# Sparse attention block: 76 instead of 64 of the 128 query blocks gather their selected rows from memory

## The chip, the cores and the metric

One NeuronCore of a Trainium2 chip. The metric is the device time of one execution of the whole kernel in microseconds (us), as the median of several runs. One execution was also recorded by the hardware profiler; every row below is from it.

## The reference, cut to what matters

The model is x = x + 0.5 FFN(LN(x)); x = x + Attention(LN(x)); x = x + 0.5 FFN(LN(x)) on x of shape (2, 1024, 128). Only the attention is touched by the change. Its heart:

```python
I = einsum('bts,h->bts', relu(einsum('bthd,bsd->bths', q_i, k_i)), idx_w)
I = where(local, inf, I); I = where(causal, -inf, I)     # local: last 64 positions
_, idx = top_k(I, 96)                                    # 64 local ones and 32 chosen ones
key_c = (c_kv @ W_uk)[bi, idx]; value = (c_kv @ W_uv)[bi, idx]
kr_sel = (x @ W_kr)[bi, idx]; key_r = pope(kr_sel, angles_k)
scores = (q_c . key_c + q_r . key_r) * scale
out = softmax(scores) @ value
```

Each query attends to its 64 last positions and to 32 earlier ones that are picked by an index score (positions below 96 are taken in a fixed order where fewer exist).

## The kernel before, in words

**Stages.** The span of 1686.8 us holds an FFN stage, the attention, and the FFN stage again. The attention has a start of its own up to about 687 us (projections, selection for the first tiles), and then a loop over 128 blocks of 16 queries up to about 1139 us. The change lies in the loop and, with one list, in that start.

**Blocks, tiles, phases.** A tile is 128 queries, 8 blocks k = 0 to 7. A batch has 8 tiles: the near ones are its tiles 0 to 3, the far ones 4 to 7. The loop has 8 phases q = 0 to 7 (q = 0 to 3 for batch 0) of 16 blocks. A phase takes one far tile and one near tile (`far_tile`, `near_tile`: near tiles 3, 2, 1, 0 in turn), in pairs of blocks: two far, two near, two far, and so on (`place`). So r, the place in the phase, is 2, 3, 6, 7, 10, 11, 14, 15 for the near blocks, and 14 and 15 are their k = 6 and 7.

**The 32 chosen rows of a block** reach the transposed keys (`pe_keys`) in one of two ways. Far blocks: GpSimd issues 4 indirect DMAs (L750) that fetch rows of `kv_rows` from memory into one of GR = 6 buffers `G`, and TensorE transposes the four (L1136). Near blocks: VectorE makes one-hot matrices (`dve_onehot`, L1886), one for each 128 candidate positions (`chunks`: 1 to 4), and TensorE multiplies a three-part bf16 table of all keys with them (L1142, three matmuls for each one-hot); for the value product the fetched rows are then turned back by four transposes (L1173 in `pe_turned`), which gathered blocks don't need.

**The loop** is software pipelined. In its iteration i, TensorE does in this order: `pe_turned`(i) (L1170), `pe_keys`(i+3), `pe_scored`(i+2) (L1155, L1158, L1161), the index units that are due, `pe_mixed`(i) (L1186, L1189). VectorE: `dve_inverse`(i+1) (L1908), `dve_keys`(i+3) (L1894), `dve_least`(i+2) (L1903), `dve_onehot`(i+5), every fourth time `dve_attended` (L1918), and the selection steps due. ScalarE: `act_turned`(i) (L1422), `act_queries` (L1412), `act_scaled`(i+1) (L1435), `act_weights`(i+2) (L1429), the index units due (`act_index`). Each engine takes them strictly in this order; I count iterations by TensorE's L1170. The key work of near blocks at r = 14 and 15 is therefore in the iterations at r = 11 and 12.

**Selection** for a tile list s = 2q (far) or 2q + 1 (near) is spread over the phase before its own. `INDEX` lists TensorE's units with their iteration: index scores (L1123, four heads for each half of 512 positions) and, for far lists, a transpose of the finished list (half None, L1117), whose result ScalarE copies with four instructions to `IDX` (L1393), from which GpSimd's gathers read. All units share two PSUM banks: `pe_index` lets unit v wait until ScalarE has handled unit v-2.

```python
v = IX_AT[s, half, h]
if v >= 2:
    pe.wait_ge(ix_out, v - 1)
o = bank[v % 2]
```

With B = 16(q-1) - 4, far list 2q has its units at B-5 to B-2 and its transpose at B+7; near list 2q+1 has its scores at B+4 and B+5. `STEPS` lists VectorE's: "add0" and "add1" sum the heads (L1840), eleven steps find the 32 largest (L1871, L1873, L1875), "out" writes the list. So at r = 9 VectorE has the "out" of a near list and then "add0" of the next far list, and at r = 10 TensorE has two index units, of heads 2 and 3 of the second half. The near list goes through memory to all partitions (`sp_near`), for the one-hots. GpSimd's gather of far block d waits for the last use of its buffer (`ob_done` of the far block six earlier).

Of the kernel before, what the change touches and what calls it, by code (L numbers as in the profile page):

```python
# [16 lines left out]
P = 128  # L17
# [56 lines left out]
    return q, far, (far_tile if far else near_tile)(q), 2 * (r // 4) + r % 2  # L74


def position(d):

    q, k = divmod(d, 8)
    return q * PER + 4 * (k // 2) + k % 2  # L80


def chunks(tile, k):
# [4 lines left out]
def onehots():  # L88

    units = []  # L90
    for i in range(NB):
        q, far, tile, k = place(i)
        if not far:
            units += [(i, c) for c in range(chunks(tile, k))]
    return units

# [9 lines left out]
def index_units():  # L106

    units = []
    for q in range(PHASES):
        base = PER * (q - 1) - SHIFT  # L110
        for half in range(2):
            units += [(base - 5 + 2 * half + h // 2, 2 * q, half, h) for h in range(NIH)]
        units += [(base + 4 + h // 2, 2 * q + 1, 0, h) for h in range(NIH)]
        units += [(base + 7, 2 * q, None, None)]
    return sorted(units, key=lambda u: u[0])


# [9 lines left out]
    return sorted(steps, key=lambda u: u[0])  # L127


ONEHOTS = onehots()  # L130
OH_AT = {i: [n for n, u in enumerate(ONEHOTS) if u[0] == i] for i in range(NB)}
INDEX = index_units()
# [102 lines left out]
def build(nc, ins, const_ap, rot_ap, mask_ap, out):  # L235
# [10 lines left out]
    with ExitStack() as ctx:  # L246
# [55 lines left out]
        inverse = sb("inverse", [P, 3])  # L302
        best = sb("best", [P, NSEL])
        bidx = sb("bidx", [P, NSEL], U32)
        bidf = sb("bidf", [P, 2, NSEL])
        bidh = sb("bidh", [P, 2, NSEL], F16)
        near0 = sb("near0", [P, NSEL])
        IDX = sb("IDX", [P, PHASES, P // 4], U32)

        arena_at = -(-nc.sbuf_base // 32) * 32  # L310
# [134 lines left out]
        mus_done, qr_ready = sem("mus_done"), sem("qr_ready")  # L445
        q_placed = [sem(f"q_placed{i}") for i in range(2)]

        ix_done, ix_out, sc_used, far_ready, near_ready, idx_ready = (sem(n) for n in ("ix_done", "ix_out", "sc_used", "far_ready", "near_ready", "idx_ready"))
        idx_stored, oh_ready = sem("idx_stored"), sem("oh_ready")
        idxb_loaded = [sem(f"idxb_loaded{half}") for half in range(2)]  # L450
        gathered = [sem(f"gathered{i}") for i in range(GR)]
# [271 lines left out]
        def pool_sel(pool):  # L723
            pool_rstd(pool, 3)
            pool.wait_ge(x_ready, 1)
            pool.wait_ge(xn_ready, NG * 2)
            pool.memset(KVS[:, :, ROWKV:], 1.0)
            pool.drain()
            pool.memset(KL[0:P // 2, :, :], 0.0)
            pool.memset(KL[P // 2:, :, 0:LW], 0.0)  # L730
            pool.drain()
            pool.memset(RT[P // 2:, :], 1.0)
            pool.wait_ge(mask_loaded, 16)
            pool.drain()
            pool.tensor_copy(maskb[:, :, :].rearrange("p v n -> p (v n)"), MASKF)
            pool.drain()
            pool.memset(spare[:, 10:11], 0.0).then_inc(padded, 1)
            pool.wait_ge(kv_stored, 16 * B)
            for q in range(PHASES):
                for k in range(8):  # L740
                    d = 8 * q + k
                    if d == 4:
                        pool.wait_ge(qr_ready, 2 * 2 * B)
                    if d >= GR:
                        pool.wait_ge(ob_done, position(d - GR) + 1)
                    if k == 0:
                        pool.wait_ge(idx_ready, 3 * (q + 1))
                        pool.wait_ge(ix_out, IX_AT[2 * q, None, None] + 1)
                    for g in range(GB):
                        pool.indirect_dma_start(G[d % GR][:, g, :], None, kv_rows,  # L750
                                                bass.IndirectOffsetOnAxis(ap=IDX[:, q, k * GB + g:k * GB + g + 1], axis=0))\
                            .then_inc(gathered[d % GR], 16)

        def pe_turn(pe, tile, n, ready, base):

# [227 lines left out]
        def pe_sel(pe):  # L983
# [63 lines left out]
            pe_raw_queries(pe, 3)  # L1047
            pe_swap(pe, 2)
            pe_swap(pe, 3)
            for u in INDEX:  # L1050
                if u[0] < 0 and u[1] == 2:
                    pe_index(pe, u)
# [55 lines left out]
        def pe_index(pe, unit):  # L1108

            _, s, half, h = unit  # L1110
            v = IX_AT[s, half, h]
            if v >= 2:
                pe.wait_ge(ix_out, v - 1)
            o = bank[v % 2]
            if half is None:
                pe.wait_ge(far_ready, s // 2 + 1)
                pe.transpose(o[0:NSEL, 0:P], bidf[:, s // 2 % 2, :], ident).then_inc(ix_done, 1)  # L1117
                return
            tile = tile_of(s)
            b = tile // TB  # L1120
            r = slice((h % 2) * DH, (h % 2 + 1) * DH)
            lo, hi = half * BANK, min(scores_of(s), (half + 1) * BANK)
            pe.matmul(o[:, 0:hi - lo], QI[r, h // 2, tile * P:(tile + 1) * P], KI[r, b * L + lo:b * L + hi],  # L1123
                      start=True, stop=True).then_inc(ix_done, 1)

        def pe_keys(pe, x):

            q, far, tile, k = place(x)
            if x >= 2:
                pe.wait_ge(gts_ready, x - 1)  # L1130
            o = bank[4 + x % 2]
            if far:
                d = 8 * q + k
                pe.wait_ge(gathered[d % GR], 16 * GB * (d // GR + 1))
                for g in range(GB):
                    m = pe.transpose(o[:, g * P:(g + 1) * P], G[d % GR][:, g, :], ident)  # L1136
            else:
                b, n = tile // TB, chunks(tile, k)
                for c in range(n):
                    pe.wait_ge(oh_ready, OH_AT[x][c] + 1)  # L1140
                    for part in range(OHPARTS):
                        m = pe.matmul(o[:, :], TAB[part][:, 4 * b + c, :], OH[OH_AT[x][c] % OHR][:, :],  # L1142
                                      start=(c == 0 and part == 0), stop=(c == n - 1 and part == OHPARTS - 1))
            m.then_inc(gt_done, 1)
# [18 lines left out]
        def pe_turned(pe, x):  # L1163
# [4 lines left out]
                pe.wait_ge(pts_ready, x)  # L1168
            for part in range(2):
                m = pe.transpose(bank[6][:, part * P:(part + 1) * P], PB[x % 3][:, part * P:(part + 1) * P], ident)  # L1170
            if not far:
                for g in range(GB):
                    m = pe.transpose(bank[6][:, 2 * P + g * DC:2 * P + (g + 1) * DC],  # L1173
                                     GTS[x % 3][2 * DR:ROWKV, g * P:(g + 1) * P], ident[2 * DR:ROWKV, 2 * DR:ROWKV])
            m.then_inc(tp_done, 1)

        def pe_mixed(pe, x):
# [7 lines left out]
            pts = PTS[x % 2]  # L1185
            pe.matmul(o, KVS[:, tile, 2 * DR:ROWKV] if k >= 4 else KV64[:, tile, :], pts[:, 0:P], start=True, stop=True)  # L1186
            for g in range(GB):
                rows = G[(8 * q + k) % GR][:, g, 2 * DR:ROWKV] if far else pts[:, 2 * P + g * DC:2 * P + (g + 1) * DC]
                m = pe.matmul(o[:, g * STRIP:(g + 1) * STRIP], rows, pts[:, P + g * STRIP:P + (g + 1) * STRIP],  # L1189
                              start=False, stop=True, skip_group_check=True)  # L1190
            m.then_inc(ob_done, 1)
# [103 lines left out]
        def act_sel(act):  # L1295
# [49 lines left out]
            for n in range(B, 2 * B):  # L1345
                act_round(act, n)
                act_log(act, (MU[n % 2],)).then_inc(mu_log, 1)
            for u in INDEX:
                if u[0] < 0 and u[1] == 2:
                    act_index(act, u)  # L1350
# [32 lines left out]
        def act_index(act, unit):  # L1383
# [3 lines left out]
            act.wait_ge(ix_done, v + 1)  # L1387
            o = bank[v % 2]
            if half is None:
                q = s // 2  # L1390
                src = o[0:NSEL, 0:P].rearrange("p (g t) -> p t g", t=4)
                for t in range(4):
                    m = act.activation(IDX[t * NSEL:(t + 1) * NSEL, q, :], src[:, t, :], ACT.Copy)  # L1393
                    m.then_inc(ix_out if t == 3 else idx_ready, 1)
                return
            n = min(scores_of(s), (half + 1) * BANK) - half * BANK
# [17 lines left out]

        def act_turned(act, x):

            far = place(x)[1]
            act.wait_ge(tp_done, x + 1)
            if x >= 2:
                act.wait_ge(ob_done, x - 1)  # L1420
            n = 2 * P if far else 3 * P
            act.activation(PTS[x % 2][:, 0:n], bank[6][:, 0:n], ACT.Copy).then_inc(pts_ready, 1)  # L1422

        def act_weights(act, x):
# [401 lines left out]
        def dve_select(dve, unit):  # L1826
# [15 lines left out]
                                             ALU.mult, ALU.add).then_inc(sc_used, 2 if h == 1 else 1)  # L1842
                return
            if step == "out":
                f = bidf[:, q % 2, :]
                if s % 2 == 0:
                    if q >= 2:
                        dve.wait_ge(ix_done, IX_AT[s - 4, None, None] + 1)
                    dve.tensor_copy(f, bidx[:, :])
                    dve.drain()  # L1850
                    dve.tensor_scalar(f, f, float(tile // TB * L), None, ALU.add).then_inc(far_ready, 1)
# [4 lines left out]
                if tile % TB == 0:  # L1856
                    dve.tensor_copy(near0[:, :], bidx[:, :])
                    dve.drain()
                    dve.tensor_tensor(near0[:, :], near0[:, :], cst("keep"), ALU.mult)
                    dve.drain()  # L1860
                    dve.tensor_tensor(fh, near0[:, :], cst("fill"), ALU.add).then_inc(near_ready, 1)
                else:
                    dve.tensor_copy(fh, bidx[:, :]).then_inc(near_ready, 1)
                return
            r = slice(step // 3 * 8, step // 3 * 8 + 8)
            if step == 0:
# [10 lines left out]
        def dve_onehot(dve, x):  # L1877

            q, far, tile, k = place(x)
            if far:  # L1880
# [132 lines left out]
```

## Time and profile before

| | |
|---|---|
| median of 3 runs | 1689.7 us (1689.04 to 1690.89) |
| the profiled execution | 1688.96 us, its span 1686.8 us |
| PE (TensorE matmul) busy | 1401.3 us, 83% of the span |
| DVE (VectorE) | 1243.8 us, 74% |
| ACT (ScalarE) | 976.6 us, 58% |
| POOL (GpSimd) | 447.8 us, 27% |
| the 128-block loop | about 687 to 1139 us |

Busy time counts the latency of single instructions, and matmuls overlap: a row of nine matmuls of 395 ns each does not last nine times as long. Spacing, the distance from one step's start to the next's, is what counts on TensorE. "PEclk" is the clock granted to TensorE as a share of full speed. "Idle before" names what ended an engine's wait.

### The profile page before, as it was taken

The numbers are of one execution on the slowest core, as the hardware profiler recorded it, in microseconds if no ns is written. First come the engines' busy times: TensorE is split into PE (matmuls) and PEld (weight loads), VectorE is DVE, ScalarE is ACT, GpSimd is POOL, SyncE is SP. The second block draws the span as 40 slices with busy tenths as digits, with TensorE's granted clock in tenths as the row PEclk, the third lists the DMA queues.
The fourth block names the chain that finished last, engine by engine and source line by source line (L and its number), as shares of the span: only waits on it lengthen the run. The fifth ranks groups of instructions, "written<-read, shape, count | busy, mean of one in ns | idle before, by whom it ended". The sixth has DMA issues, their size and how long they took to land.

```text
span 1686.8 us, 31737 instructions
## 1 busy us (share of the span) xinstructions
PE 1401.3 (83%) x10664; PEld 915.3 (54%) x10664; DVE 1243.8 (74%) x2568; ACT 976.6 (58%) x1788; POOL 447.8 (27%) x751
## 2 busy tenths in 40 slices
PE   3599999799994754789999989996399999799994
PEld 2355554577773311456656655675255555577773
DVE  4578886698778577677878887754478887488787
ACT  2166666478883672346455555552166666488883
POOL 4122222100002023245455445622222233100000
PEclk9599999799997965899899999997599999799998
DMA  5211110022202244122122122212311110022200
GB/s 143 95 48 45 43 47 11 1 102 76 75 26 78 47 121 112 30 61 61 36 80 73 38 61 63 74 36 81 110 33 47 46 47 18 2 102 75 75 25 25
DMA packets 65020, 99.72 MB, mean 59 GB/s; under 512 B 21109, under 2 KB 44853, under 8 KB 62840
## 3 DMA queue, kind: packets, MB, share of 16 engines
q1 hardware_dynamic: 55254, 80.43, 15.5%
q0 software_dynamic: 8192, 16.79, 3.9%
q8 instruction: 75, 1.23, 0.3%
q10 hardware_dynamic: 1440, 0.80, 0.2%
q14 instruction: 59, 0.47, 0.1%
HBM read 73.39 MB, written 10.69 MB: 50 GB/s over the span
## 4 chain that ended last, share of the span: by engine, by line
PE 55%; DVE 13%; ACT 10%; DMA 6%; issue 6%; SPq 5%; DVEq 4%; ACTq 1%; POOL 0%; POOLq 0%
PE twin L973 8%; PE twin L963 5%; PE twin L827 5%; PE twin L1142 5%; PE twin L805 5%; DMA ffn<-arena 4%; PE twin L772 4%; ACT arena L1209 4%; DVEq L1830 2%; ACT experts L1279 2%; PE twin L1170 2%; PE twin L1158 2%; PE twin L1123 2%; PE twin L1186 2%; ACT arena L1277 2%
## 5 line engine op out<-in xcount | busy, mean ns | idle before, releaser
L1209 ACT ACTIVATE arena<-twin 128x1024 f32<-128x1024 f32 x288 | 293.8, 1024 | 172.7 <-PE twin L805 170.8
L750 POOL DMA_INDIRECT arena<-kv_rows,IDX x256 | 251.6, 983 | 309.9 <-PE twin L1189 151.0
L1478 DVE TENSOR_REDUCE arena<-twin 128x8 f32<-128x1024 f32 (+1 forms) x160 | 195.3, 1225 | 77.2 <-PE twin L772 42.9
L1277 ACT ACTIVATE arena<-twin,bias 128x512 f32<-128x512 f32 x256 | 184.9, 722 | 60.6 <-PE twin L963 60.6
L1527 DVE TENSOR_TENSOR experts<-arena,experts 128x512 fp32r<-128x512 f32 x256 | 170.1, 689 | 61.8 <-ACT experts L1279 60.5
L963 PE MATMUL twin<-experts,experts 128*128 128x512 f32 x768 | 197.0, 403 | 6.1 <-ACT experts L1279 6.1
L772 PE MATMUL twin<-ffn,ffn 64*128 64x128 f32 (+3 forms) x1152 | 154.8, 351 | 50.5 <-DMA arena<-arena 27.7
L1468 DVE TENSOR_REDUCE arena<-twin 128x2 f32<-128x1024 f32 x128 | 152.9, 1222 | 51.8 <-PE twin L772 48.4
L1279 ACT ACTIVATE experts<-twin,bias 128x512 fp32r<-128x512 f32 x256 | 186.2, 727 | 0.0
L973 PE MATMUL twin<-experts,experts 128*128 128x512 f32 x768 | 183.3, 390 | 1.0 <-DVE experts L1527 1.0
L711 POOL TENSOR_SCALAR_AFFINE_SELECT arena<-arena 128x256 f32<-128x256 f32 x256 | 99.6, 407 | 307.6 <-ACT arena L1209 307.6
L805 PE MATMUL twin<-ffn,ffn 64*128 64x128 f32 (+3 forms) x960 | 148.4, 373 | 27.7 <-DMA ffn<-arena 22.7
L963 PEld LDWEIGHTS twin<-experts,experts 128*128 128x128 f32 x768 | 143.2, 192 | 51.1 <-ACT experts L1279 23.7
L973 PEld LDWEIGHTS twin<-experts,experts 128*128 128x128 f32 x768 | 143.9, 188 | 32.9 <-issue 2.6
L827 PE MATMUL twin<-arena 128*32 128x128 f32 (+3 forms) x1920 | 159.2, 432 | 2.6 <-POOL arena L711 1.6
L645 POOL TENSOR_TENSOR rstd<-vareps,neghalf 128x8 f32<-128x8 f32 x14 | 23.4, 1674 | 511.7 <-DVE vareps L1457 511.7
L772 PEld LDWEIGHTS twin<-ffn,ffn 64*128 64x128 f32 x1152 | 96.7, 201 | 83.9 <-ACT arena L1209 36.1
L805 PEld LDWEIGHTS twin<-ffn,ffn 64*128 64x128 f32 x960 | 79.2, 188 | 109.0 <-issue 62.4
L1894 DVE TENSOR_TENSOR HN<-twin,RT 96x512 f32<-96x512 f32 x128 | 86.9, 680 | 59.1 <-PE twin L1142 51.4
L1429 ACT ACTIVATE ATT<-twin,col 128x256 f32<-128x256 f32 x128 | 60.6, 473 | 104.9 <-DVE col L1903 104.0
L1435 ACT ACTIVATE ATT<-ATT,inverse 128x256 f32<-128x256 f32 x128 | 64.6, 505 | 81.3 <-DVE inverse L1908 80.8
L1142 PE MATMUL twin<-XN,arena 128*128 128x512 bf16 x408 | 104.2, 395 | 0.2 <-DVE HN L1894 0.2
(258 smaller groups left out, 2186.6 us busy)
## 6 DMA issues: line engine op xcount, KB each, us to landing
arena<-wt_rows SPq DMA_DIRECT2D x16, 1024.0 KB, 4.8
arena<-in_L_ffn_w SPq DMA_DIRECT2D x32, 256.0 KB, 5.2
ffn<-q_rows SPq DMA_DIRECT2D x64, 128.0 KB
ffn<-k_rows SPq DMA_DIRECT2D x64, 128.0 KB
XT<-idx_rows SPq DMA_DIRECT2D x16, 512.0 KB, 4.1
q_rows<-ffn SPq DMA_DIRECT2D x8, 512.0 KB, 4.9
k_rows<-ffn SPq DMA_DIRECT2D x4, 1024.0 KB, 9.2
arena<-HN SPq DMA_DIRECT2D x32, 128.0 KB, 2.4
```

The source lines that it names most:

```text
L750: pool.indirect_dma_start(G[d % GR][:, g, :], None, kv_rows, bass.IndirectOffsetOnAxis(ap=IDX[:, q, k * GB + g:k * GB + g + 1], axis=0))\
L772: m = pe.matmul(bank[2 * slot + s][:, at * P:(at + blocks) * P], QB[buf][r, q * P:(q + 1) * P], KB[buf][r, k0 * P:(k0 + blocks) * P], star ...
L805: x = pe.matmul(bank[2 * slot + s][:, at * P:(at + 4 - p) * P], KB[buf][r, kc * P:(kc + 1) * P], QB[buf][r, (4 * g + p) * P:(4 * g + 4) * ...
L827: m = pe.matmul(bank[6][r:r + STRIP, p * P:], VS[buf][:, v:v + STRIP], PT[(UNITS * buf + u) % PT_RING][:, s, at * P:(at + 4 - p) * P], sta ...
L963: m = pe.matmul(bank[f][:, :], W1R[buf][w][:, f * P:(f + 1) * P], XR[x][:, tb * BANK:(tb + 1) * BANK], start=((w, x) == pairs[0]), stop=(( ...
L973: m = pe.matmul(bank[4 + k][:, :], W2R[buf][w][:, f, :], H1R[k][x][:, f, :], start=(f == 0 and (w, x) == pairs[0]), stop=(f == FC - 1 and ...
L1142: m = pe.matmul(o[:, :], TAB[part][:, 4 * b + c, :], OH[OH_AT[x][c] % OHR][:, :], start=(c == 0 and part == 0), stop=(c == n - 1 and part ...
L1209: act.activation(PT[(UNITS * buf + u) % PT_RING].rearrange("p s n -> p (s n)"), twin[2 * u % S_RING][:, :], ACT.Exp, scale=float(HD) ** -0 ...
L1277: act.activation(H1[tb % 2][:, f, :], bank[f][:, :], ACT.Gelu_apprx_tanh, bias=bias1[buf][:, f:f + 1])
L1279: act.activation(H1R[tb % 2][0][:, f, :], bank[f][:, :], ACT.Gelu_apprx_tanh, bias=bias1[buf][:, f:f + 1]).then_inc(gelu_done, 1)
L1478: dve.tensor_reduce(to, scores.rearrange("p (s t k) -> p s t k", s=2, t=to.shape[2]), AX_X, ALU.max).then_inc(max_done, 1)
L1527: dve.tensor_tensor(H1R[tb % 2][1][:, f, :], H1[tb % 2][:, f, :], H1R[tb % 2][0][:, f, :].bitcast(F32), ALU.subtract)\
```

## The change

Near blocks k = 6 and 7 of every near tile with at least two chunks there, that is near tiles 3, 2 and 1 of both batches (phases 0, 1, 2, 4, 5, 6), are gathered from memory as far ones are: 12 blocks more, 76 of 128. Their one-hots, table matmuls and the four transposes in `pe_turned` go. For this the near lists too are turned into row numbers: "out" of a near list makes them in `bidf` (with the batch's offset added), and each near list gets a transposing unit in `INDEX` and its four copies to `IDX`. The gathers run through one list `GATHERED`; their buffers are handed on from one gathered block to the one six places later in that list.

```diff
+def gathered_rows(i):
+    q, far, tile, k = place(i)
+    return far or (k >= 6 and chunks(tile, k) >= 2)
...
-        units += [(base + 7, 2 * q, None, None)]
+        units += [(base + 7, 2 * q, None, None), (base + (14 if q else 7), 2 * q + 1, None, None)]
...
+GATHERED = [i for i in range(NB) if gathered_rows(i)]
+G_AT = {i: d for d, i in enumerate(GATHERED)}
...
+            lists = set()
+            for d, i in enumerate(GATHERED):
+                q, far, tile, k = place(i)
+                s = 2 * q + (0 if far else 1)
...
+                if d >= GR:
+                    pool.wait_ge(ob_done, GATHERED[d - GR] + 1)
+                if s not in lists:
+                    lists.add(s)
+                    pool.wait_ge(idx_ready, 3 * (s + 1))
+                    pool.wait_ge(ix_out, IX_AT[s, None, None] + 1)
...
             pe_swap(pe, 3)
+            pe_index(pe, INDEX[IX_AT[1, None, None]])
...
-            if far:
-                d = 8 * q + k
+            if gathered_rows(x):
+                d = G_AT[x]
...
                 act_log(act, (MU[n % 2],)).then_inc(mu_log, 1)
+            act_index(act, INDEX[IX_AT[1, None, None]])
...
+                f = bidf[:, s % 4, :]
+                if q >= 2:
+                    dve.wait_ge(ix_done, IX_AT[s - 4, None, None] + 1)
+                dve.tensor_copy(f, bidx[:, :])
+                dve.drain()
+                if tile % TB == 0:
...
+                dve.tensor_copy(fh, f).then_inc(near_ready, 1)
+                dve.drain()
+                dve.tensor_scalar(f, f, float(tile // TB * L), None, ALU.add).then_inc(list_ready, 1)
                 return
```

In the `INDEX` that results, the transpose of near list 2q+1 (q from 1) falls into iteration 16q - 6, the place r = 10, and stands there ahead of the two index units of far list 2q+2.

## Rows read from the trace of the kernel before

**Rows 1.** The page's chain that ended last, by engine.
```profile
PE 55%; DVE 13%; ACT 10%; DMA 6%; issue 6%; SPq 5%; DVEq 4%; ACTq 1%; POOL 0%; POOLq 0%
```
**Rows 2.** Windows of iterations 113 to 116: us, then PE PEld DVE ACT POOL busy, PEclk.
```profile
1101.26:1103.44 2.18, 2.18 (x30) 1.70 (x27) 1.98 (x6) 1.37 (x5) 1.53 (x2) 1.00 0.32 79
1103.44:1106.14 2.70, 2.70 (x34) 2.01 (x32) 1.54 (x5) 1.76 (x6) 2.09 (x3) 1.00 0.29 76
1106.14:1109.00 2.86, 2.86 (x34) 1.91 (x31) 1.53 (x4) 1.45 (x5) 2.02 (x3) 1.00 0.32 76
1109.00:1111.39 2.39, 2.39 (x29) 1.64 (x26) 1.32 (x4) 1.57 (x6) 1.89 (x2) 1.00 0.33 78
```
**Rows 3.** Windows of iterations 75 to 77 of phase 4, same columns.
```profile
971.14:975.94 4.80, 4.80 (x42) 2.79 (x39) 2.63 (x8) 2.75 (x8) 2.93 (x4) 1.00 0.82 252
975.94:980.28 4.34, 4.34 (x38) 2.53 (x36) 2.87 (x7) 1.69 (x6) 0.00 (x0) 1.00 0.08 27
980.28:984.33 4.05, 2.26 (x31) 1.71 (x28) 3.78 (x8) 1.37 (x4) 2.84 (x3) 1.00 0.14 36
```
**Rows 4.** Timeline of iteration 74 (r = 10): start, us, engine, line; ScalarE's index unit last.
```profile
966.41 1.13 DVE L1886 TENSOR_SCALAR XN<-XT,const 128x512 bf16<-128x512 f16 x4
967.63 0.18 DVE L1863 CAST bidh<-bidx 128x32 f16<-128x32 uint32 x1
969.41 1.21 PE L1123 MATMUL twin<-arena 64*128 64x320 f32 x4
971.90 0.94 ACT L1400 ACTIVATE arena<-twin,aw 128x320 f32<-128x320 f32 x2
```
**Rows 5.** Timeline around iteration 67: a far list's transpose and its four copies.
```profile
942.84 0.27 PE L1117 MATMUL twin<-const,bidf 128*32 128x128 f32 x1
944.15 0.80 ACT L1393 ACTIVATE IDX<-twin 32x32 uint32<-32x32 f32 x4
```
**Rows 6.** DVE timeline of phase 4: its waits for near keys in iterations 75 and 76.
```profile
974.67 0.69 DVE L1894 TENSOR_TENSOR HN<-twin,RT 96x512 f32<-96x512 f32 x1 [2.01 <-PE twin L1142]
979.01 0.69 DVE L1894 TENSOR_TENSOR HN<-twin,RT 96x512 f32<-96x512 f32 x1 [0.69 <-PE twin L1142]
```
**Rows 7.** The same of phase 1 (iteration 27).
```profile
800.36 0.69 DVE L1894 TENSOR_TENSOR HN<-twin,RT 96x512 f32<-96x512 f32 x1 [2.18 <-PE twin L1142]
```
**Rows 8.** Timeline of phase 3, iterations 58 and 59.
```profile
908.54 0.59 PE L1123 MATMUL twin<-arena 64*128 64x192 f32 x4
909.65 0.44 PE L1170 MATMUL twin<-const,ATT 128*128 128x128 f32 x2
910.45 0.72 ACT L1400 ACTIVATE arena<-twin,aw 128x192 f32<-128x192 f32 x2
911.24 0.69 DVE L1894 TENSOR_TENSOR HN<-twin,RT 96x512 f32<-96x512 f32 x1 [0.50 <-PE twin L1142]
```
**Rows 9.** Chain of waits from 590 to 700 us: the near list's cast stands on it.
```profile
625.37 0.28 DVE bidh L1863
```
**Rows 10.** Timeline at the end of the attention's start: DVE's wait there.
```profile
678.95 1.57 DVE L1719 MEMSET HN<- 32x512 f32 x3 [2.83 <-DMA arena<-XN]
```
**Rows 11.** POOL timeline: first and last gather of the third-last pair of blocks (8 instructions).
```profile
1091.46 0.94 POOL L750 DMA_INDIRECT arena<-kv_rows,IDX  x1 [1.42 <-PE twin L1189]
1100.19 0.94 POOL L750 DMA_INDIRECT arena<-kv_rows,IDX  x1 [0.30 <-issue]
```
**Rows 12.** Windows of iterations 18 (phase 1) and 82 (phase 5), the same work.
```profile
764.81:768.88 4.07, 4.07 (x32) 2.90 (x32) 3.60 (x11) 3.15 (x10) 2.85 (x5) 0.60 0.21 50
999.77:1003.10 3.33, 2.84 (x31) 2.01 (x31) 3.24 (x11) 2.77 (x9) 2.42 (x4) 1.00 0.20 48
```
**Rows 13.** All gather instructions of L750 by source: duration min/median/max in ns.
```profile
L750 POOL DMA_INDIRECT arena<-kv_rows,IDX x256: 938/944/1897, 619.4 to 1110.3; - x128
```
**Rows 14.** The page's DMA issues: KB each, and us from issue to landing.
```profile
XT<-idx_rows SPq DMA_DIRECT2D x16, 512.0 KB, 4.1
arena<-HN SPq DMA_DIRECT2D x32, 128.0 KB, 2.4
```

More of the change, by code:

```diff
@@ L74, in place @@
     return q, far, (far_tile if far else near_tile)(q), 2 * (r // 4) + r % 2
-def position(d):
-    q, k = divmod(d, 8)
-    return q * PER + 4 * (k // 2) + k % 2
+def gathered_rows(i):
+    q, far, tile, k = place(i)
+    return far or (k >= 6 and chunks(tile, k) >= 2)
 def chunks(tile, k):
@@ L92, in onehots @@
         q, far, tile, k = place(i)
-        if not far:
+        if not gathered_rows(i):
             units += [(i, c) for c in range(chunks(tile, k))]
@@ L304, in build @@
         bidx = sb("bidx", [P, NSEL], U32)
-        bidf = sb("bidf", [P, 2, NSEL])
+        bidf = sb("bidf", [P, 4, NSEL])
         bidh = sb("bidh", [P, 2, NSEL], F16)
-        near0 = sb("near0", [P, NSEL])
         IDX = sb("IDX", [P, PHASES, P // 4], U32)
@@ L446, in build @@
         q_placed = [sem(f"q_placed{i}") for i in range(2)]
-        ix_done, ix_out, sc_used, far_ready, near_ready, idx_ready = (sem(n) for n in ("ix_done", "ix_out", "sc_used", "far_ready", "near_ready", "idx_ready"))
+        ix_done, ix_out, sc_used, list_ready, near_ready, idx_ready = (sem(n) for n in ("ix_done", "ix_out", "sc_used", "list_ready", "near_ready", "idx_ready"))
         idx_stored, oh_ready = sem("idx_stored"), sem("oh_ready")
@@ L738, in pool_sel @@
             pool.wait_ge(kv_stored, 16 * B)
-            for q in range(PHASES):
-                for k in range(8):
-                    d = 8 * q + k
[L742 to L752, printed above, removed]
+            lists = set()
+            for d, i in enumerate(GATHERED):
+                q, far, tile, k = place(i)
+                s = 2 * q + (0 if far else 1)
+                if d == 4:
+                    pool.wait_ge(qr_ready, 2 * 2 * B)
+                if d >= GR:
[4 more added lines that the diff above has]
+                    pool.wait_ge(ix_out, IX_AT[s, None, None] + 1)
+                for g in range(GB):
+                    pool.indirect_dma_start(G[d % GR][:, g, :], None, kv_rows,
+                                            bass.IndirectOffsetOnAxis(ap=IDX[:, s % PHASES, k * GB + g:k * GB + g + 1], axis=0))\
+                        .then_inc(gathered[d % GR], 16)
         def pe_turn(pe, tile, n, ready, base):
@@ L1115, in pe_index @@
             if half is None:
-                pe.wait_ge(far_ready, s // 2 + 1)
-                pe.transpose(o[0:NSEL, 0:P], bidf[:, s // 2 % 2, :], ident).then_inc(ix_done, 1)
+                pe.wait_ge(list_ready, s + 1)
+                pe.transpose(o[0:NSEL, 0:P], bidf[:, s % 4, :], ident).then_inc(ix_done, 1)
                 return
@@ L1131, in pe_keys @@
             o = bank[4 + x % 2]
-            if far:
-                d = 8 * q + k
+            if gathered_rows(x):
+                d = G_AT[x]
                 pe.wait_ge(gathered[d % GR], 16 * GB * (d // GR + 1))
@@ L1170, in pe_turned @@
                 m = pe.transpose(bank[6][:, part * P:(part + 1) * P], PB[x % 3][:, part * P:(part + 1) * P], ident)
-            if not far:
+            if not gathered_rows(x):
                 for g in range(GB):
@@ L1187, in pe_mixed @@
             for g in range(GB):
-                rows = G[(8 * q + k) % GR][:, g, 2 * DR:ROWKV] if far else pts[:, 2 * P + g * DC:2 * P + (g + 1) * DC]
+                rows = G[G_AT[x] % GR][:, g, 2 * DR:ROWKV] if gathered_rows(x) else pts[:, 2 * P + g * DC:2 * P + (g + 1) * DC]
                 m = pe.matmul(o[:, g * STRIP:(g + 1) * STRIP], rows, pts[:, P + g * STRIP:P + (g + 1) * STRIP],
@@ L1389, in act_index @@
             if half is None:
-                q = s // 2
                 src = o[0:NSEL, 0:P].rearrange("p (g t) -> p t g", t=4)
                 for t in range(4):
-                    m = act.activation(IDX[t * NSEL:(t + 1) * NSEL, q, :], src[:, t, :], ACT.Copy)
+                    m = act.activation(IDX[t * NSEL:(t + 1) * NSEL, s % PHASES, :], src[:, t, :], ACT.Copy)
                     m.then_inc(ix_out if t == 3 else idx_ready, 1)
@@ L1415, in act_turned @@
         def act_turned(act, x):
-            far = place(x)[1]
             act.wait_ge(tp_done, x + 1)
@@ L1420, in act_turned @@
                 act.wait_ge(ob_done, x - 1)
-            n = 2 * P if far else 3 * P
+            n = 2 * P if gathered_rows(x) else 3 * P
             act.activation(PTS[x % 2][:, 0:n], bank[6][:, 0:n], ACT.Copy).then_inc(pts_ready, 1)
@@ L1844, in dve_select @@
             if step == "out":
-                f = bidf[:, q % 2, :]
-                if s % 2 == 0:
[L1847 to L1851, printed above, removed]
+                f = bidf[:, s % 4, :]
[4 more added lines that the diff above has]
+                if tile % TB == 0:
+                    dve.tensor_tensor(f, f, cst("keep"), ALU.mult)
+                    dve.drain()
+                    dve.tensor_tensor(f, f, cst("fill"), ALU.add)
+                    dve.drain()
+                if s % 2 == 0:
+                    dve.tensor_scalar(f, f, float(tile // TB * L), None, ALU.add).then_inc(list_ready, 1)
                     return
@@ L1855, in dve_select @@
                     dve.wait_ge(idx_stored, 16 * (q - 1))
[L1856 to L1863, printed above, removed]
+                dve.tensor_copy(fh, f).then_inc(near_ready, 1)
+                dve.drain()
+                dve.tensor_scalar(f, f, float(tile // TB * L), None, ALU.add).then_inc(list_ready, 1)
                 return
@@ L1879, in dve_onehot @@
             q, far, tile, k = place(x)
-            if far:
+            if gathered_rows(x):
                 return
```

## The prediction

> **What bounds the kernel now.** I read the page first. The chain that ended last lies on TensorE for 55% and on VectorE for 13%, on GpSimd not at all [rows 1]. So the question is what the 128-block loop makes of less TensorE work, and I read it iteration by iteration in windows that run from one first instruction of `pe_turned` to the next. Late in the loop, when selection is over, TensorE fills each window: 2.18 or 2.70 us for an iteration that transposes gathered rows, 2.86 or 2.39 us for one that builds near keys from one chunk [rows 2]. The two of each kind differ by 0.5 us: that is the value transposes L1173, which only a near block has. In phase 4 the iterations at r = 11 and 12, which build the keys of near blocks k = 6 and 7 from four chunks, last 4.80 and 4.34 us with TensorE full, and VectorE is busy for 2.63 and 2.87 us of them; the next one has TensorE busy for 2.26 of 4.05 us and VectorE for 3.78 [rows 3]. So TensorE bounds r = 11 and 12, VectorE bounds what follows, and both take work in strict order, so a delay at r = 10 or 11 is handed on to both. That is where I look closest, because the change also adds a unit at r = 10.
>
> **What is removed.** Three chunks more cost 4.80 - 2.86 = 1.94 us, so a chunk costs 0.65 us. With gathered rows, r = 11 and 12 take 2.70 + 2.18 = 4.88 us [rows 2]. Against 9.14 us for four chunks [rows 3] TensorE can give back 4.26 us in phases 0 and 4, 4.26 - 1.30 = 2.96 us in phases 1 and 5 (three chunks), 1.67 us in phases 2 and 6 (two): 17.8 us in all. The L1173 transposes at r = 14 and 15 give 0.5 us each, but only where TensorE bounds: in phase 6, 1.0 us. VectorE loses 36 one-hots; four took 1.13 us [rows 4], so 4, 3 or 2 of them stand at r = 9 and as many at r = 10. In r = 11 VectorE waited 2.01 us for the near keys in phase 4 and 0.69 us more in r = 12 [rows 6], and 2.18 us in phase 1 [rows 7]; what TensorE gives back is worth these waits and little more.
>
> **What is added at r = 10.** The near list's transpose is put ahead of the two index units there. Before, unit v waited for ScalarE to have done unit v-2, and with two units in an iteration those were units of the iteration before. With three, the last one waits for the list's unit of the same iteration. ScalarE comes to its index units only at the end of its own iteration, after `act_weights`: in iteration 74 TensorE issued the two units from 969.41 us on, the second at about 969.8, and ScalarE began them at 971.90 [rows 4]. It will now first make the four copies of the list, 0.80 us [rows 5]. Behind the waiting unit stand `pe_mixed` and the whole next iteration, and VectorE then waits for the next keys.
> - Phases 0 and 4: four one-hots go ahead of ScalarE's start (-1.13 us) and two small operations come in "out" (one takes 0.18 us and with its drain 0.26, so +0.52), so it starts at 971.3. 971.3 + 0.80 + 0.05 = 972.15, minus 969.8: TensorE stands 2.35 us. In r = 11 gathered keys reach VectorE 1.27 us into the iteration instead of 974.67 - 971.14 = 3.53 [rows 3, 6], 2.26 us saved, so VectorE is 0.1 us late there; the wait of 0.69 us in r = 12 goes. Net -0.6 us each, -1.2.
> - Phases 1 and 5: a stall of 2.3 us, a saving of 2.26 - 0.65 = 1.61 us, no second wait to save: +0.7, and 0.15 for the later scores. +0.85 us each, +1.7.
> - Phase 2: a stall of about 2.9 us (two one-hots fewer, but two operations more), a saving of 0.97 us and perhaps a second wait of the size of the 0.69: between +0.5 and +1.9. I take +1.0.
> - Phase 3 gathers nothing more, but has the added unit too. The two units start at 908.54 and about 908.7, ScalarE at 910.45 and then 0.5 later: 910.45 + 0.52 + 0.85 - 908.7 = 3.1 us. VectorE's only wait there was 0.50 us and was for the keys themselves [rows 8], so nothing absorbs it: +3.1 us.
> - Phase 6 has the list alone at r = 10, no stall: -1.67 - 1.0 + 0.2 for the transpose = -2.5 us.
>
> **GpSimd's supply.** Eight gathers took from 1091.46 to 1100.19 + 0.94 us, 1.25 us a step, so 10.0 us for a pair of blocks; four iterations take 10.1 us [rows 2, 11]. Before, a buffer came free 12 iterations ahead of its next block; after six gathered blocks in a row it is 8. The tightest place is r = 5 of phase 7: from the first release of the pair to the use of its second block are five iterations of 2.18, 2.18, 2.39, 2.39 and 2.18 us and 0.7 more, 12.0 us; the eighth gather starts 0.6 + 8.75 = 9.35 us after it. The trace has no row for a gather's landing. With 2.4 us it is in time, with 4.1 us [rows 14] it is 1.45 us late. I take the middle, +0.7 us. In the other phases iterations are 3.5 us and more, and the slack is above 4 us.
> Most gather instructions take 944 ns, the longest 1897 [rows 13]. The Trainium skill ("SBUF — State Buffer", section "SBUF: two separate sides") says that VectorE operations of certain modes lock GpSimd out of a shared port while it writes descriptors, which speaks against putting more gathers beside a full VectorE. By it the supply would cost nearer 1.45 than 0.7 us; by the rows few instructions are stretched, and they are in phases with slack.
>
> **The attention's start.** "out" of near list 0 stands on the chain as one cast of 0.28 us [rows 9] and becomes three operations: +0.5 us. The added transpose and copies (about 1 us) delay the selection for list 2, which ends in a wait of VectorE of 2.83 us for a DMA [rows 10]: hidden. If that cover were gone they would cost 1 us.
>
> **TensorE's clock.** Iteration 18 had a granted clock of 0.60, that is partly 1.2 GHz, and took 4.07 us; iteration 82, the same work at 1.00 (2.4 GHz), took 3.33 [rows 12]. Such falls come after iterations like 77, where TensorE is half idle. Work is removed and stalls are added ahead of just these, so I add two such falls, +1.5 us; the ends are 0 and 3.
>
> **Sum.** 0.5 - 1.2 + 1.7 + 1.0 + 3.1 - 2.5 + 0.7 + 1.5 = +4.8 us on the profiled execution of 1688.96 us (its span of 1686.8 and 2.2 around it), 1693.8 us. The median of the runs shown lies 0.7 us above that execution: 1694.5 us. With the ends of the terms (phases 0 and 4 -1.4 to +0.4 each, 1 and 5 +0.4 to +1.5, phase 2 +0.5 to +1.9, phase 3 +2.3 to +3.6, phase 6 and supply -2.5 to -1.0, start 0.3 to 0.8, clock 0 to 3), not all at one side, the forecast's own range is 1691 to 1699 us.
>
> **The rivals.**
> *Faster: the added unit doesn't hold TensorE.* If ScalarE reaches the list early, because VectorE, freed of the one-hots, lets it run ahead, the savings come through: 3.6 us in phases 0 and 4 (between the waits of 2.7 us of rows 6 and TensorE's 4.26), 2.5 in 1 and 5, 1.7 in 2, +0.2 in 3, and -1.8 and +0.5 as above: -15 us, 1674.7 us. For it: TensorE bounds and loses 17.8 us of work. Against: ScalarE was 2.1 us behind TensorE's second unit [rows 4], and the one-hots are worth only 0.6 us of that. It decides where that lag falls under about 0.5 us. Half of it would be 1684.
> *Slower still: the clock.* If each of the six stalls brings two iterations at the low clock, 6 x 2 x 0.74 = 8.9 us stand in place of 1.5: 1701.9 us. For it: TensorE's share of the time falls just ahead of its idle iterations. Against: phase 4 went through the same iterations at 1.00 throughout [rows 3]. The Trainium skill ("TensorE: Matmul & The Clock Gate", section "HAM oscillation — how this bites in real kernels") says that gaps between bursts of matmuls take the clock back again and again; by it this rival is the likelier one, by the rows 0.74 us a time is all it costs.
> *Slower: gathers late.* If every pair of phase 7 lands late by 1.45 us, 4.4 us stand in place of 0.7: 1698.2 us. It decides from a landing of 2.65 us on.
>
> **How the numbers follow.** Forecast 0.60, faster rival 0.17, clock 0.13, late gathers 0.06, 0.04 for a small gain or loss. No change is within 0.2%, 3.4 us, about what a measurement of this kernel can tell. The forecast's 4.8 us lie just above: 0.42 slower and 0.18 the same. The faster rival is 0.15 faster and 0.02 the same, both others slower, the rest the same: 0.15, 0.24, 0.61. The range goes from 1684, half of the faster rival, to 1701, most of the clock's.
>
> **What would show it.** In the new trace L1123 at r = 10 should have a wait on ScalarE's copies (L1393's line), 2.3 to 3 us, in phases 0 to 5 and not in 6; the windows r = 11 and 12 should be 2.7 and 2.2 to 2.5 us; L1886 should have 100 instructions and the gathers 304; phase 3 should be longer by 3 us, phase 6 shorter by 2. The prediction is wrong if phase 3 is not longer, or if GpSimd's gathers are waited for before phase 6.

## The result and the profile after

The changed kernel takes 1704.6 us in the median (1702.6 to 1708.2), the kernel before on the same chip 1690.1 us (1689.0 to 1690.9). The ratio is 1.0089, with an interval of 1.0069 to 1.0109: 14.6 us slower, where I had forecast 4.8 slower and a range up to 1701. The profiled execution took 1702.62 us with a span of 1700.9, the longer by 14.1 us. The first `pe_turned` is 1.04 us later than before, the loop is 11.5 us longer (441.4 to 452.9), and the rest 1.5 us.

The chain of the page, in the place of [rows 1], still lies on TensorE first:

```profile
PE 51%; DVE 16%; ACT 10%; DMA 7%; issue 7%; DVEq 4%; SPq 3%; POOL 1%; ACTq 0%; POOLq 0%
```

TensorE's waits in the loop: engine, line, releaser, us in total, times, the longest.

```profile
PE twin L1174 <- ACT ATT L1438: 31.0, 27, 2.4
PE twin L1127 <- ACT IDX L1397: 12.8, 6, 2.9
PE twin L1140 <- DMA arena<-kv_rows,IDX: 1.0, 1, 1.0
```

The second row is the predicted wait, which I call the hold: at r = 10 of phases 0 to 5 the last index unit (L1127, before L1123) waits for ScalarE's copies of a near list (L1397). The third is the only time that TensorE waited for a gather in the loop. (The first row was there before, with 25.4 us in 24 waits.) The timeline of iteration 58, phase 3, shows one hold; it answers to [rows 8]:

```profile
912.14 0.73 ACT L1404 ACTIVATE arena<-twin,aw 128x192 f32<-128x192 f32 x2 [1.52 <-DVE arena L1843]
912.64 0.27 PE L1121 MATMUL twin<-const,bidf 128*32 128x128 f32 x1
912.93 0.59 PE L1127 MATMUL twin<-arena 64*128 64x192 f32 x2
914.76 0.47 ACT L1432 ACTIVATE ATT<-twin,col 128x256 f32<-128x256 f32 x1 [0.41 <-DVE col L1906]
915.23 0.80 ACT L1397 ACTIVATE IDX<-twin 32x32 uint32<-32x32 f32 x4
916.08 1.00 PE L1127 MATMUL twin<-arena 64*128 64x192 f32 x2 [2.56 <-ACT IDX L1397]
917.01 0.63 PE L1190 MATMUL twin<-ATT,arena 128*32 128x128 f32 x2
```

The list's transpose and the first unit are done by 913.5. ScalarE still has its own iteration to finish, up to `act_weights` at 914.76, and only then copies the list. The last unit starts 0.05 us after the copies. A unit of the same shape takes 0.59 us ahead of the hold and 1.00 us behind it: the granted clock fell to half at 915.78, 0.30 us before the hold's end. Windows of r = 10 and 11 in phases 1 and 3, of r = 10, 11 and 12 in phase 4, and of r = 11, 12 in phase 6 (us, then PE PEld DVE ACT POOL busy, PEclk), to be held beside [rows 3]:

```profile
795.29:801.67 6.38, 4.77 (x39) 2.62 (x36) 3.41 (x7) 4.54 (x13) 4.86 (x6) 1.00 0.56 211
801.67:804.37 2.70, 2.70 (x35) 2.01 (x32) 1.11 (x2) 1.68 (x5) 0.69 (x1) 1.00 0.21 64
910.63:918.00 7.37, 4.80 (x39) 3.20 (x37) 4.08 (x10) 4.36 (x14) 5.85 (x6) 0.85 0.57 178
918.00:922.81 4.81, 4.48 (x32) 2.83 (x31) 1.32 (x3) 1.28 (x4) 1.25 (x2) 0.52 0.18 54
977.44:983.82 6.38, 4.34 (x39) 2.62 (x36) 3.53 (x8) 4.34 (x13) 4.86 (x6) 1.00 0.71 206
983.82:988.21 4.39, 4.39 (x34) 3.11 (x31) 1.41 (x3) 1.93 (x6) 0.90 (x1) 0.53 0.18 52
988.21:991.57 3.36, 3.36 (x30) 2.53 (x28) 2.53 (x7) 1.36 (x6) 0.00 (x0) 0.60 0.01 2
1098.59:1101.28 2.69, 2.69 (x34) 2.00 (x31) 1.27 (x3) 1.96 (x9) 1.92 (x3) 1.00 0.68 119
1101.28:1103.47 2.19, 2.19 (x30) 1.71 (x28) 1.30 (x4) 1.58 (x6) 1.74 (x2) 1.00 0.99 386
```

In phase 1 the clock stays at 1.00 and r = 11 takes the predicted 2.70 us. In phase 4 the same work takes 4.39 us at 0.53, and r = 12 takes 3.36 instead of 2.19. So it is in five of the six phases, all but phase 1: behind the hold TensorE runs at its lower level, 1.2 GHz, and with it goes most of what r = 11 and 12 saved (in phase 4, 9.14 us became 7.75 and not 4.88). Phase 6, with no hold, keeps it: 3.51 + 3.04 us became 2.69 + 2.19.

One of these five falls is not new. The kernel before has one of 3.4 us in the same phase, at r = 11 of phase 2, where no index unit waits; in the changed kernel one of 10.2 us begins in the hold there. These are its windows of r = 11 in phase 2 and in phase 6, which have the same work, keys from two chunks:

```profile
856.73:861.79 5.06, 5.06 (x33) 2.69 (x34) 2.12 (x6) 2.12 (x8) 2.98 (x4) 0.66 0.77 257
1084.57:1088.07 3.50, 3.50 (x36) 2.19 (x33) 1.86 (x5) 1.47 (x5) 2.59 (x4) 1.00 0.54 145
```

### The profile page after: what moved, and what is told of

It reads as the page before. It is cut to its first block, busy times and chain, and to the rows that moved or that the text cites. A ratio compares the mean times of both kernels' runs of the same rounds, so it can differ in the third digit from the quotient of the medians.

```text
span 1700.9 us, 31587 instructions
## 1 busy us (share of the span) xinstructions
PE 1388.4 (82%) x10536; PEld 913.5 (54%) x10564; DVE 1237.9 (73%) x2548; ACT 982.9 (58%) x1820; POOL 492.0 (29%) x799
## 4 chain that ended last, share of the span: by engine, by line
PE 51%; DVE 16%; ACT 10%; DMA 7%; issue 7%; DVEq 4%; SPq 3%; POOL 1%; ACTq 0%; POOLq 0%
PE twin L976 8%; PE twin L830 5%; PE twin L966 5%; PE twin L808 5%; DMA ffn<-arena 4%; PE twin L775 4%; ACT arena L1213 3%; PE twin L1146 3%; DVEq L1833 3%; ACT experts L1283 2%; PE twin L1174 2%; PE twin L1127 2%; PE twin L1162 2%; ACT arena L1281 2%; PE twin L1190 1%
## 5 line engine op out<-in xcount | busy, mean ns | idle before, releaser
L753 POOL DMA_INDIRECT arena<-kv_rows,IDX x304 | 295.5, 972 | 288.5 <-PE twin L1193 108.0
L830 PEld LDWEIGHTS twin<-arena 128*32 128x32 f32 x1920 | 56.6, 109 | 75.9 <-issue 58.9
```

The source lines that it names most:

```text
L753: pool.indirect_dma_start(G[d % GR][:, g, :], None, kv_rows, bass.IndirectOffsetOnAxis(ap=IDX[:, s % PHASES, k * GB + g:k * GB + g + 1], a ...
L830: m = pe.matmul(bank[6][r:r + STRIP, p * P:], VS[buf][:, v:v + STRIP], PT[(UNITS * buf + u) % PT_RING][:, s, at * P:(at + 4 - p) * P], sta ...
```

## The experiments

The theory: each hold costs its own length, and the low clock behind it more on top; the gathers by themselves are a gain. The rival: the loss comes with the gathers or with the added work wherever it stands, and the clock's falls are chance. All changes below are to the changed kernel.

**The groups of runs.** Each group has runs of the kernel before beside the others. In the first two groups, with seven runs of the kernels below, the kernel before took 1818 and 1807 us in the median, 7 to 8% more than the 1690 of the result; in the two later ones, with five, it took 1689 us. The first two were on the chips with the numbers 12 and 0, the later ones on 8 and 0, so a slow and a normal group bear the same number, and I can't say whether the difference belongs to a chip or to a time. I compare within a group, and read the sizes from the later groups. The changed kernel itself ran in none of the later ones: where I set one of them beside its 1704.6 us, the baselines differ by up to 0.9 us.

### The list's transpose one iteration later

```diff
-        units += [(base + 7, 2 * q, None, None), (base + (14 if q else 7), 2 * q + 1, None, None)]
+        units += [(base + 7, 2 * q, None, None), (base + (15 if q else 7), 2 * q + 1, None, None)]
```

In the first two groups:

> The changed kernel with the near lists' transposing unit one iteration later, at r = 11, where no other index unit stands; nothing else differs. Theory (the added unit at r = 10 makes TensorE wait for ScalarE's copies, and the wait takes its clock down): no wait of L1127 for L1397, r = 10 as before (3.8 us in phase 4), r = 11 and 12 of 2.7 and 2.2 us at full clock; 1672 to 1684 us, about 26 us under the changed kernel. Rival (the added gathers cost: GpSimd or the memory traffic holds the loop): the wait goes, but the time stays above 1697 us, with TensorE waiting for gathers.

> The near list's transpose stands one iteration later, at r = 11, where no other index unit is; all else as in the changed kernel. Theory: the holds of TensorE at r = 10 (about 2 to 3 us, six of them) and the half-clock stretches behind them go, 25 to 30 us below the changed kernel, about 1675 to 1682 us if the kernel before takes 1690, or 0.5 to 0.9 % below it. Rival (the holds only take the place of waits that VectorE or ScalarE would cause anyway): within 0.2 % of the changed kernel.

Measured 1839.8 us, ratio 1.0118 (1.0072 to 1.0164), and 1841.1 us, ratio 1.0193 (1.0173 to 1.0214). Beside the changed kernel of the same group (1854.0, below) it is 12.9 us faster, in the sign of the theory and half its size. But it is slower than the kernel before, as the rival had it; the waits for gathers that the rival named too are not among those recorded. Then in a later group:

> Once more the near list's transpose at r = 11 instead of r = 10, all else as in the changed kernel, because TensorE on the chip of the two groups of runs before stood still for 1 to 4 us some 35 times in the loop, in the kernel before as well (1807 us there instead of 1690). On a chip without those stops: theory (the holds at r = 10 and the low clock behind them are more than the whole loss) 1672 to 1684 us; rival (the loss comes with the gathers) over 1697 us.

Measured 1680.6 us, 0.9958 of the kernel before (0.9938 to 0.9978), 24 us below the changed kernel (22 us by the ratios). Its waits have no row in which L1127 waits for L1397. Its windows of r = 10 to 12 in phase 4, and of r = 10 and 11 in phase 3:

```profile
960.89:964.34 3.45, 3.45 (x39) 2.33 (x36) 3.11 (x7) 2.14 (x5) 2.84 (x3) 1.00 0.49 112
964.34:967.68 3.34, 2.87 (x35) 2.02 (x32) 2.08 (x5) 2.98 (x8) 2.43 (x4) 1.00 0.96 305
967.68:969.87 2.19, 2.19 (x31) 1.71 (x28) 2.00 (x6) 1.92 (x9) 0.82 (x1) 1.00 0.27 66
...
900.88:904.66 3.78, 3.48 (x38) 2.50 (x35) 3.33 (x8) 1.93 (x6) 3.17 (x3) 1.00 0.29 82
904.66:907.75 3.09, 3.05 (x32) 1.93 (x32) 1.98 (x6) 2.66 (x8) 2.17 (x4) 1.00 0.87 296
```

Three iterations of 8.98 us instead of 14.13, all at full clock, with the same gathers beside them. The place of one transpose in each phase made a gain into a loss.

### The list's transpose at r = 13

> The near list's transpose at r = 13, where TensorE is half idle, instead of r = 10; all else as in the changed kernel. Theory: no hold, and the 0.3 us of the transpose no longer lies in r = 11, which TensorE bounds: the same as with r = 11 or up to 3 us below it. Rival (ScalarE's four copies of 0.8 us then delay the keys of r = 14 to 0, which wait for selection): up to 5 us above it.

Measured 1681.5 us, 0.9946 (0.9924 to 0.9967), no different from r = 11. Both places clear of the units of r = 10 do. Its profiled loop has 47.8 us at the lower clock against 27.3 with r = 11, nearly all of it between r = 13 of a phase and r = 4 of the next, and is 4.5 us longer; the medians, over more executions, differ by 0.9 us.

### The lists alone, without the gathers

```diff
-    return far or (k >= 6 and chunks(tile, k) >= 2)
+    return far
```

> The changed kernel, but only far blocks are gathered (64 as before): the near lists are still turned into row numbers, transposed at r = 10 and copied, and nobody reads them. Theory: the whole loss and nothing of the gain. Phase 3 of the changed kernel, which had no new gathers, became 6.1 us longer; six such phases, the start's 1.0 us: 1710 to 1727 us, the lower end if the clock stays up. Rival (gathers cost): 1691 to 1693 us.

> Only the far blocks gather, as before, but every near list is still made into row numbers, transposed at r = 10 and copied by ScalarE. Theory (the list's unit at that place is the whole loss): it has the holds and no savings, so it is 1.2 to 2.2 % slower than the kernel before, more than the changed kernel is. Rival (the loss comes with the twelve further gathered blocks, their gathers on GpSimd and their DMA traffic): within 0.2 % of the kernel before.

> Only the far blocks gather, as before, with the near lists' rows, transposes at r = 10 and copies kept, for a chip without the stops. Theory (these units are the whole loss, and the twelve further gathers a gain): 1710 to 1727 us, more than the changed kernel. Rival (the loss comes with the gathers): within 0.2 % of 1690 us.

First two groups: 1834.9 us, 1.0092 (1.0059 to 1.0126), and 1825.4 us, 1.0106 (1.0082 to 1.0129). The second is a miss: it was to be slower than the changed kernel and is 28.7 us faster (1854.0). Later group: 1722.7 us, 1.0209 (1.0167 to 1.0251), 33.6 us above the kernel before and 18 above the changed one. TensorE's wait is the same, and each of the six now has a stretch of low clock that begins in it or up to 1.2 us behind it, with nothing saved in return (phase 4, r = 10 to 12):

```profile
PE twin L1127 <- ACT IDX L1397: 13.1, 6, 2.9
...
989.55:998.25 8.70, 5.62 (x39) 3.21 (x36) 5.37 (x15) 4.66 (x14) 5.80 (x6) 0.80 0.54 165
998.25:1004.55 6.30, 6.30 (x41) 3.31 (x39) 1.11 (x2) 1.18 (x4) 0.00 (x0) 0.74 0.05 18
1004.55:1008.89 4.34, 4.34 (x38) 2.53 (x36) 2.86 (x7) 1.70 (x6) 0.00 (x0) 1.00 0.00 0
```

### The lists alone, at r = 11

Both edits together.

> As the last one (64 gathered blocks, near lists turned into row numbers), but with the list's unit at r = 11. Theory: no wait in the loop; what is left is the start's 1.0 us and 0.2 us for each transpose: 1691 to 1693 us. If turning the lists into row numbers costs by its own work (VectorE's two added operations, ScalarE's four copies), and not by the wait: above 1697 us.

> Only the far blocks gather, and the near lists' transposes stand at r = 11, for a chip without the stops. Theory: no hold, so the added transposes, copies and VectorE operations alone cost 1 to 3 us: 1691 to 1693 us. Rival (the added work itself costs, wherever it stands): over 1697 us.

First group: 1814.5 us, 0.9975 (0.9943 to 1.0008), with one execution of ten at 4167 us. Later group: 1695.1 us, 1.0042 (1.0024 to 1.0059), between the two expectations. Without the hold the added work costs 6 us instead of 33.6. In the loop I can show 4.4 us of it at r = 10 to 12 of phases 0 to 5 (the loop as a whole is 3.2 longer): r = 10 of phase 4 takes 4.74 us where it took 3.83 before, and 0.5 to 0.6 more in the others, which is about the size of the operations added to "out".

```profile
968.22:972.96 4.74, 3.92 (x39) 2.60 (x36) 3.85 (x10) 2.14 (x5) 3.83 (x4) 1.00 0.25 72
972.96:977.87 4.91, 4.91 (x43) 2.81 (x41) 2.64 (x9) 2.87 (x8) 1.98 (x3) 1.00 0.72 246
```

### The hold filled with matmuls

TensorE makes 36 matmuls in the hold, whose results the next `pe_mixed` overwrites. The hold stays; TensorE is busy in it. (The expectations call them 64x128; by the trace 32 weight columns are loaded, 128*32. A first form that wrote to a bank from which ScalarE reads has no time on record.)

```diff
+                due = [u for u in INDEX if u[0] == i]
+                for n, u in enumerate(due):
+                    if n == 2:
+                        o = bank[7][i // 4 % 4 * DC:(i // 4 % 4 + 1) * DC, i % 4 * P:(i % 4 + 1) * P]
+                        for f in range(36):
+                            pe.matmul(o, ident_b[:, 0:DC], ident_b[:, :], start=True, stop=True)
+                    pe_index(pe, u)
```

> As the changed kernel, but ahead of the third index unit of an iteration TensorE makes 36 matmuls of 64x128 whose results are overwritten, about 1.9 us at full clock, inside the hold of 2 to 3 us. The hold stays as long, TensorE is busy in it. Theory (the hold itself costs half of the loss, the low clock after it the other half): the half-clock stretches behind r = 10 go, and it is 6 to 11 us below the changed kernel. Rival (the clock falls for another reason, or costs nothing): within 0.2 % of the changed kernel, or up to 5 us above it.

> The filled hold once more, for a chip without the stops: TensorE makes 36 overwritten matmuls of 64x128 (about 1.9 us at full clock) inside each hold of 2 to 3 us at r = 10. Theory (a hold costs its own 2 to 3 us less what it would have saved, and five of six also bring 6.8 us or more at half clock, worth about 2 us each): the half-clock stretches that begin at a hold's end go, 6 to 11 us below the changed kernel, 1694 to 1699 us. Rival (the clock falls for another reason, or costs nothing): within 0.2 % of the changed kernel's 1704.6 us or above it.

Second group: 1864.1 us, 1.0308 (1.0287 to 1.0329), 10 us above the changed kernel, a miss; there the clock falls all through the loop, with or without a hold (242 us of 608 at the lower level). Later group: 1696.3 us, 1.0044 (1.0026 to 1.0062), 8.3 us below the changed kernel (7.6 by the ratios), as the theory had it. Timeline of iteration 74, then windows of r = 10 to 12 (lines are 4 higher here, L1131 for L1127):

```profile
975.70 2.18 PE L1081 MATMUL twin<-ident_b 128*32 128x128 bf16 x36
976.96 0.80 ACT L1401 ACTIVATE IDX<-twin 32x32 uint32<-32x32 f32 x4
977.82 0.80 PE L1131 MATMUL twin<-arena 64*128 64x320 f32 x2
...
972.75:979.14 6.39, 6.39 (x76) 4.63 (x73) 3.53 (x8) 4.33 (x13) 4.87 (x6) 1.00 0.72 213
979.14:981.83 2.69, 2.69 (x34) 2.00 (x32) 1.11 (x2) 1.51 (x5) 0.90 (x1) 1.00 0.25 67
981.83:984.44 2.61, 2.26 (x30) 1.71 (x27) 2.32 (x6) 1.67 (x5) 0.08 (x1) 1.00 0.00 0
```

r = 10 of this phase is as long as in the changed kernel (6.39 and 6.38 us), r = 11 takes 2.69 instead of 4.39. In phases 1 and 5, which have the shortest holds (1.6 us), the 2.2 us of filling outlast them: r = 10 is 6.81 there against 6.38. Behind none of the six holds has the clock fallen. It still falls elsewhere, from r = 13 of a phase to r = 2 of the next: the loop has 37.5 us at the lower level, against 61.4 in the changed kernel and 34.1 before.

### The changed kernel in the second group

> The changed kernel itself, so that its profile stands beside the others of the same chip. Theory (the added unit at r = 10 holds TensorE 2 to 3 us in phases 0 to 5, and each hold lets its clock fall for the iterations behind it): the six holds and at least four of the half-clock stretches that begin at their end come back, and the time is 12 to 17 us above the kernel before. Rival (the falls of the clock were chance of one recorded execution): the holds come back, but two or fewer of the stretches, and the profiled span is shorter than the first one by 5 us or more.

Measured 1854.0 us, 1.0255 (1.0234 to 1.0277): 46.6 us above the kernel before, where 12 to 17 were expected. Neither expectation fits, since another thing covers the loop there: 607.7 us for the loop, 269.7 of them at the lower clock. Its waits show engines that stand for a signal that no recorded instruction gives:

```profile
DVE HN L1897 <- remote: 82.2, 29, 5.5
ACT ATT L1425 <- remote: 79.0, 32, 4.3
DVE HN L1897 <- PE twin L1140: 32.8, 16, 5.7
```

For example, the last transpose of iteration 6 is recorded at 726.66 us, and its signal to ScalarE comes at 730.85. What holds it back is open; no run takes it apart, and there is no profile of the kernel before in these groups. Two of their results stand by themselves: moving the list gained there too (12.9 us, second group), but the gathered blocks lost. With the list at r = 11 the kernel with gathers had 1.0118 and the one without 0.9975 in the first group, about 25 us for the twelve blocks, where in the later groups they gained 14.5. Why is open as well.

## Why the prediction was wrong

The step that failed is the term for TensorE's clock. I had taken two more falls and 1.5 us; the falls at the holds cost 12.7 us where they stand and about 8 in the whole kernel. To show it I add up r = 10 to 12 over phases 0 to 5, in us, from one profiled execution each (the changed kernel's was the shortest of its four runs):

| kernel | r = 10 to 12, phases 0 to 5 | loop | median |
|---|---|---|---|
| before | 70.1 | 441.4 | 1689 to 1690 |
| changed | 84.9 | 452.9 | 1704.6 |
| list at r = 11 | 55.5 | 428.0 | 1680.6 |
| hold filled | 72.2 | 445.4 | 1696.3 |
| lists alone, r = 10 | 101.8 | 474.7 | 1722.7 |
| lists alone, r = 11 | 74.6 | 444.6 | 1695.1 |

- **The hold: right.** It is at the place and between the two engines that I predicted, and nearly as long: 1.6 to 2.9 us each, 12.8 together, where my six (2.35, 2.3, 2.9, 3.1, 2.35, 2.3) make 15.3. Its own price is the filled kernel less the one with the list at r = 11: 72.2 - 55.5 = 16.7 us, 2.8 each (about 0.9 us of the 16.7 is filling that outlasts two of the holds). My terms for these iterations in phases 0 to 5 (-1.2, +1.7, +1.0, +3.1) sum to +4.6; with the clock kept up it is 72.2 - 70.1 = +2.1, and the whole loop is 4.0 us longer.
- **TensorE's clock: the step that failed.** I took +1.5 us, with 3 as the end. The runs show 84.9 - 72.2 = 12.7 us at r = 10 to 12; other places give 5.2 back, so it is 7.5 us in the loop and 8.3 in the median. That is 6 to 7 of the 9.8 us by which the forecast was short; 0.5 us more at the start, 1.5 after the loop and 1.2 in the loop with the clock kept up are most of the others. Two mistakes are in the term. I assumed two more falls, although TensorE now stood still before its densest iterations in six phases; five of six holds have one, of which four are new. And I priced a fall at 0.74 us for an iteration, from [rows 12], an iteration that TensorE doesn't fill at full clock (2.84 of 3.33 us), and with the clock low for part of it only (0.60). In r = 11 TensorE is the bound: the 2.70 us of the filled kernel are 4.4 to 4.6 in the changed one, and 2.86 became 4.81 in phase 3. The trace of before had a nearer price that I passed over: its own fall at r = 11 of phase 2 made 3.5 us into 5.06, so 1.5 us for one fall. I had this rival, at 1701.9 us, with a chance of 0.13, and held [rows 3] against it. But there the iterations at full clock had no gap ahead of them (TensorE was busy for all 3.83 us of r = 10), so they said nothing of the case. The Trainium skill ("TensorE: Matmul & The Clock Gate", section "HAM oscillation — how this bites in real kernels") tells of a kernel that waits for DMA between bursts of matmuls and whose clock is taken back each time. Its waits are longer than the holds here, so my sentence that by it this rival was the likelier claimed too much; the trace shows falls with shorter waits too: one of 2.56 us, and then an iteration of 4.81 us at 0.52. What sets a fall off, these runs don't show in full: in phase 1 a hold of 1.61 us brought none, in phase 5 one of 1.62 us did.
- **Phase 3:** +3.1 predicted, +6.1 measured. Here no saving hides the clock. With the hold filled, phase 3 is 56.1 us, 2.0 above before; the other 4.1 us go with the clock.
- **Phase 6:** -2.5 predicted, -0.7 measured. r = 11 and 12 gave 1.7 us as predicted, and the L1173 transposes their 1.0 at r = 14 and 15, but one gather came late there and took 1.2 of it (below), and two iterations at its start were 0.7 us longer.
- **Supply of gathers: near in size (0.7 predicted, 1.0 waited), wrong in place.** I looked for it in phase 7, at r = 5. It is in iteration 110, r = 14 of phase 6, for the second block of a pair, the only late one:

```profile
1107.11 0.63 PE L1140 MATMUL twin<-const,arena 128*128 128x128 f32 x4 [1.01 <-DMA arena<-kv_rows,IDX]
```

- **Gather instructions made longer by VectorE**, which the prediction weighed, did not come: they still take 944 ns in the median and 1900 at most, as in [rows 13], with 48 more of them.
- **The start: +0.5 predicted, +1.0 measured.** The other kernels, with the same start, have their first `pe_turned` 1.0 to 3.8 us later than the kernel before. I can't separate the added operations from how executions differ, since there is one profile of the kernel before.
- **The rest, +1.5 us after the loop,** doesn't seem to be of the change: the other five have 551.0 to 552.0 us there with the same code, the kernel before 551.4, the changed one 552.9.
- **The faster rival** had the savings nearly right. Its 1674.7 us assumed the hold away; with it away the runs give 1680.6. Its gain from the gathers held (14.5 us measured); it had 0.7 us for the added work, which the lists alone at r = 11 show to cost 6.0.

Of what the prediction said the trace would show, the wait at L1127 is there in phases 0 to 5 and not in 6 (though 1.6 us in phases 1 and 5, and 2.0 in 0 and 4, and not 2.3 to 3), and so are the 100 one-hots and the 304 gathers. The windows of r = 11 and 12 fit in phase 6, and r = 11 in phase 1; phase 3 is twice as much longer as said, and phase 6 is 0.7 us shorter and not 2. The two signs that I had named for being wrong, phase 3 no longer and gathers waited for before phase 6, did not come: neither would have shown the clock's price.

## What to carry to other kernels

Where units share a ring of two buffers, a third unit in one step waits for the other engine within that step: count the units of each step before one is added, and put it in a step that has none. A wait of 1.6 to 2.9 us in front of dense matmul work is to be priced with the low clock that may come with it: here 2.8 us for the wait, and for the clock 2.1 on the spot (12.7 / 6) and 1.4 in the median (8.3 / 6). Take that price from an iteration that TensorE fills, as r = 11 of phase 2 was. And when an edit has a gain and a cost, run each alone: the +14.6 us were a gain of 14.5 (1695.1 to 1680.6), 6 for the added work, and 24 for one bad place (1680.6 to 1704.6), to within 1 us.

## What the runs showed of the hardware that I had not expected

With nothing in the wait, TensorE's granted clock fell from 1.00 to half at five of six waits of 1.6 to 2.9 us in the changed kernel and at all six with the lists alone. The fall began between 2.5 us before the wait's end and 1.6 us after it, in six of these eleven cases while TensorE still waited. With 2.2 us of small matmuls in the wait it fell at none of six. Work whose result is thrown away made the kernel 8.3 us faster, though not as fast as without the wait.

The same kernel took 1689 to 1690 us in three groups of runs and 1807 to 1818 us in two others, and the twelve gathered blocks were worth -14.5 us in the former and about +25 us in the latter. A gain of under 1% found in one group need not hold in the next.
